# Re-ordering the split of x1, two VectorE slots and the start-up transfers in a fused attention and FFN kernel

## Chip, cores and metric

The kernel runs on one core of a Trainium2 chip. The metric is the device time of one execution in microseconds (us); the median of three executions is 2120.65 us, with a lowest of 2120.45 and a highest of 2123.52.

## The reference

The input `x` has shape (2, 4096, 512), all in float32. One attention-like layer is followed by one FFN, and each is followed by a residual sum and a layer norm.

```python
k = rope((x @ Wk.T) in 16 heads of 32);  v = (x @ Wv.T) in 16 heads of 32
W = eye(32) for each batch and head
for each chunk of 16 tokens:            # 256 chunks, one after the other
    z = kc @ W
    W = W - kc.T @ (z - vc) * 2 / (16 * 32)
out = (layernorm(z) * gamma + beta) @ Wo.T
x1  = layernorm(x + out)
h   = silu((x1 @ gate_w.T) * gate_s) * ((x1 @ up_w.T) * up_s)     # 1408 wide
y   = layernorm(x1 + (h @ down_w.T) * down_s)
```

## The kernel before

**Tiles, ticks, slots.** The 4096 positions are cut into 32 tiles of 128; a tile holds both batches (256 tokens) and 8 chunks. The program is a software pipeline with the order of every engine written out by hand. `run` calls `tick(t)` for t = -1 to 35 on each engine, and a tick has 16 slots `s`. In tick t the engines work on several tiles: keys and values of tile t (and, from slot 7 on, of tile t + 1), the scan of tile sc = t - 1, norm, output projection and x1 of tile o = t - 2, and the FFN of tiles f1 = t - 2 (slots 14 and 15) and f2 = t - 3 (slots 0 to 13). Every engine takes its instructions in program order, and semaphores tie the engines together.

**The scan.** In an even slot TensorE makes z of a chunk (`scan_z`, 32 small matmuls), VectorE subtracts v (`scan_err`, 4 instructions), in the odd slot TensorE adds to the state in PSUM (`scan_state`, 16 matmuls) and ScalarE copies the state out (`keep_state`, 4 instructions). ScalarE also saves z (`save_z`).

**The split into two parts.** A float32 operand is split into a rounded high part (ScalarE, `high_x`, `high_zn`, `high_x1`, `high_hid`) and the remainder (VectorE `low_x`, `low_zn`, `low_x1`; GpSimd `low_hid`). A projection (`project_k`, `project_v`, `project_o`, 12 matmuls of 512 columns) is high times high, high times low and low times high. The FFN weights are small integers, so the FFN takes two products, if the low halves of all its weights are zero: `weigh` reduces 12 pieces of the weights to a maximum on VectorE, GpSimd reduces over partitions in tick 2, and TensorE reads the result before it goes on at slot 14 of tick 2.

**The FFN.** Eleven steps m per tile: `gate_up` (16 matmuls of 256 columns into the bank `gu_acc`), ScalarE `gate` (silu), VectorE `scale_hid`, ScalarE `high_hid`, GpSimd `low_hid`, then `down` (4 matmuls of 512 columns). There is one bank `gu_acc`, so `gate_up` of step m waits for `scale_hid` of step m - 1. Step 0 is in slot 14 and needs both parts of x1 (`x1_lo_ready`); it is where a tile's FFN begins.

**x1.** VectorE adds the projection and x in slots 7 and 8 (`add_o`), takes statistics (`stats_of`, `moments_of`), GpSimd takes the inverse root (`inverse_root`), VectorE normalizes in slot 9 and transposes 32x32 blocks (`turn_x1`), four DMAs store them and one loads them back as `landed`. In slot 13 ScalarE runs `high_x1` twice. On VectorE slot 13 reads

```python
rotate(t + 1, 0)
scale_y(yd)        # down_acc times down_scale, waits for the last down
low_x1(o, 0)
low_x1(o, 1)
```

and slot 8 reads `add_o`, `stats_of`, `scan_err`, `moments_of`, `scale_hid`. Slot 2 reads `scan_err`, `turn_zn` twice, `scale_hid`, `rotate`. The normalized z goes the same way through DRAM as x1: `turn_zn`, `store_znT`, `load_znT` (SP), `high_zn` and `low_zn` in slot 5, `project_o` in slots 6 and 7.

**The start.** The FFN weights are first copied from the inputs to DRAM scratch (three DMAs of 2816 KB, `copy_ffn`, issued by ScalarE in tick -1) and loaded in tick 1 (`load_ffn`). All four projections of tile 0 go through the one bank `work`. SP stores and loads the transposed keys (`store_kT`, `load_kT`).

## Time and profile before

| what | value |
|---|---|
| median of 3 executions | 2120.65 us |
| the profiled execution, and its span | 2128.82 us, 2126.9 us |
| TensorE busy (matmul) | 1910.0 us, 90% |
| VectorE busy | 1358.6 us, 64% |
| ScalarE, GpSimd busy | 924.4 us, 650.7 us |
| mean granted TensorE clock | 0.953 |
| slices 2 to 4 of 40: granted clock in tenths | 6, 7, 9 |

The span goes from the first to the last instruction. A granted clock of 1.00 is TensorE's full speed (2.4 GHz) and 0.50 is its lower level (1.2 GHz). The idle time in square brackets at the end of a row is that of the engine just before the instruction, with what ended it.

### The profile page before, as it was taken

Reading aid. Unit: us, or ns where it says so; the run is one execution under the profiler, and the core shown is the slowest. Engines: PE = TensorE matmul, PEld = TensorE weight load, DVE = VectorE, ACT = ScalarE, POOL = GpSimd, SP = SyncE. Lnnn points to the kernel's source line nnn. Section 1 sums busy time; section 2 is a strip of 40 time slices with the busy share of each in tenths; the row PEclk is TensorE's granted clock in tenths of the full one; section 3 lists DMA queues with packets and bytes.
Section 4 is the critical chain, followed back from the end, with each engine's and each line's share of the span. In section 5 each row is a group of like instructions: output and inputs, shape, how many; then the busy total and the mean of one; then the engine's idle time right before and its main releaser. Section 6 shows DMA issues by size and latency. Waiting matters only on the chain.

```text
span 2126.9 us, 53841 instructions
## 1 busy us (share of the span) xinstructions
PE 1910.0 (90%) x21656; PEld 1500.9 (71%) x21656; DVE 1358.6 (64%) x2878; ACT 924.4 (43%) x2258; POOL 650.7 (31%) x778
## 2 busy tenths in 40 slices
PE   5548999999999999999999999999999999998887
PEld 3326777777777777777777777777777777777665
DVE  3465676667666666676676666667666666766542
ACT  2324444444444444444444444444444444444421
POOL 1012323333333333333323323332332333333222
PEclk9679999999999999999999999999999999999998
DMA  8843444554444445444434544443454444444320
GB/s 297 266 124 117 141 120 136 152 157 127 133 138 138 131 144 155 130 143 136 142 118 142 153 149 124 137 144 116 140 153 147 125 144 138 135 122 133 94 66 21
DMA packets 307978, 294.02 MB, mean 138 GB/s; under 512 B 42896, under 2 KB 256144, under 8 KB 307728
## 3 DMA queue, kind: packets, MB, share of 16 engines
q1 hardware_dynamic: 302768, 273.26, 42.7%
q10 hardware_dynamic: 4960, 17.30, 2.2%
q8 instruction: 173, 2.83, 0.6%
q14 instruction: 77, 0.63, 0.1%
HBM read 156.19 MB, written 142.87 MB: 141 GB/s over the span
## 4 chain that ended last, share of the span: by engine, by line
PE 61%; DVE 24%; DMA 5%; issue 5%; SPq 3%; POOL 1%; ACT 1%; DVEq 0%; POOLq 0%; ACTq 0%
PE gu_acc L704 26%; PE work L690 18%; PE down_acc L716 11%; DVE err L881 7%; DVE x_lo L917 4%; PE z_acc L663 3%; PE state_acc L678 3%; DVE hid L888 2%; DVE x_tok L898 2%; SPq L252 2%; DVE turned L821 2%; DVE x_tok L816 1%; DVE stats L802 1%; DMA landed<-zT_scr 1%; DMA zT_scr<-turned 1%
## 5 line engine op out<-in xcount | busy, mean ns | idle before, releaser
L443 POOL TENSOR_TENSOR hid_lo<-hid,hid_hi 128x256 fp32r<-128x256 f32 x352 | 269.2, 765 | 1013.1 <-ACT hid_hi L534 1013.1
L704 PE MATMUL gu_acc<-x_hi,gw 128*128 128x256 f32 x1408 | 400.1, 315 | 104.3 <-DVE x_lo L917 65.8
L881 DVE TENSOR_TENSOR err<-z_acc,v_rows 32x256 f32<-32x256 f32 x1024 | 429.3, 419 | 100.9 <-PE z_acc L663 65.2
L500 ACT ACTIVATE state<-state_acc 32x256 f32<-32x256 f32 x1028 | 383.7, 373 | 111.3 <-PE state_acc L678 91.5
L704 PEld LDWEIGHTS gu_acc<-x_hi,gw 128*128 128x128 f32 x1408 | 275.0, 195 | 170.0 <-DVE hid L888 74.3
L888 DVE SCALAR_TENSOR_TENSOR hid<-gu_acc,up_scale,hid 128x256 f32<-128x256 f32 x352 | 168.9, 480 | 314.8 <-ACT hid L524 311.0
L524 ACT ACTIVATE hid<-gu_acc,gate_scale 128x256 f32<-128x256 f32 x352 | 166.6, 473 | 456.9 <-PE gu_acc L704 454.9
L704 PE MATMUL gu_acc<-x_hi,uw 128*128 128x256 f32 x1408 | 364.4, 289 | 0.0
L704 PE MATMUL gu_acc<-x_lo,uw 128*128 128x256 f32 x1408 | 363.4, 289 | 0.0
L704 PE MATMUL gu_acc<-x_lo,gw 128*128 128x256 f32 x1408 | 362.5, 288 | 0.0
L716 PE MATMUL down_acc<-dw,hid_hi 128*128 128x512 f32 x704 | 282.3, 401 | 0.9 <-POOL hid_lo L443 0.9
L704 PEld LDWEIGHTS gu_acc<-x_hi,uw 128*128 128x128 f32 x1408 | 279.2, 198 | 0.0
L716 PE MATMUL down_acc<-dw,hid_lo 128*128 128x512 f32 x704 | 279.1, 397 | 0.0
L704 PEld LDWEIGHTS gu_acc<-x_lo,uw 128*128 128x128 f32 x1408 | 278.8, 198 | 0.0
L704 PEld LDWEIGHTS gu_acc<-x_lo,gw 128*128 128x128 f32 x1408 | 277.1, 197 | 0.1
L509 ACT ACTIVATE v_rows<-z_acc 128x256 f32<-128x256 f32 x256 | 97.6, 381 | 376.9 <-DVE err L881 376.9
L690 PE MATMUL work<-wk,fm 128*128 128x512 f32 x768 | 208.5, 423 | 17.2 <-DVE fm L912 17.0
L534 ACT ACTIVATE hid_hi<-hid 128x256 fp32r<-128x256 f32 x352 | 147.0, 418 | 173.7 <-DVE hid L888 172.7
L690 PE MATMUL work<-wv,fm 128*128 128x512 f32 x768 | 205.6, 411 | 6.5 <-DVE k_sin L870 6.5
L690 PE MATMUL work<-wo,fm 128*128 128x512 f32 x768 | 196.0, 404 | 8.5 <-DVE fm L902 5.8
L690 PEld LDWEIGHTS work<-wk,fm 128*128 128x128 f32 x768 | 148.5, 200 | 59.3 <-DVE fm L912 17.8
L690 PEld LDWEIGHTS work<-wv,fm 128*128 128x128 f32 x768 | 146.0, 197 | 41.9 <-DVE k_sin L870 8.7
(64 smaller groups left out, 2122.9 us busy)
## 6 DMA issues: line engine op xcount, KB each, us to landing
x_fm<-xT SPq DMA_DIRECT2D x64, 256.0 KB, 3.5
k_scr<-k_tok SPq DMA_DIRECT2D x32, 512.0 KB, 3.4
kT_scr<-turned SPq DMA_DIRECT2D x128, 128.0 KB, 2.9
kT<-kT_scr SPq DMA_DIRECT2D x32, 512.0 KB, 3.5
k_rows<-k_scr SPq DMA_DIRECT2D x512, 32.0 KB, 2.0
v_rows<-v_scr SPq DMA_DIRECT2D x512, 32.0 KB, 2.1
z_scr<-v_rows SPq DMA_DIRECT2D x32, 512.0 KB, 3.1
z_tok<-z_scr SPq DMA_DIRECT2D x512, 32.0 KB, 1.8
```

Source lines behind the costliest of these rows:

```text
L443: pool.tensor_tensor(hid_lo[m % RING][:], hid[m % 2][:], hid_hi[m % RING][:].bitcast(F32), ALU.subtract).then_inc(hid_lo_ready, 1)
L500: act.activation(state[q, :, e].rearrange("p (r g) e -> p r g e", r=2), state_acc[q, :, 0:P].rearrange("p r (g e) -> p r g e", e=HEAD), AC ...
L509: act.activation(v_rows[:, i].rearrange("p a (r c) -> p a r c", r=2), z_acc[:, :, 0:P].rearrange("p r (a c) -> p a r c", a=2), ACT.Copy).t ...
L524: act.activation(hid[m % 2][:], gu_acc[:, 0:TOK], ACT.Silu, scale=gate_scale[:, m:m + 1]).then_inc(silu_done, 1)
L534: act.activation(hid_hi[m % RING][:], hid[m % 2][:], ACT.Copy).then_inc(hid_hi_ready, 1)
L663: mm = pe.matmul(z_acc[j * HEAD:(j + 1) * HEAD, r, odd * 2 * HEAD:(odd + 1) * 2 * HEAD], lhsT=k_cols[k, i // 2, g, i % 2, :], rhs=state[k, ...
L690: mm = pe.matmul(work[:], lhsT=fm[p_x][:, c, b, :], rhs=w[p_w][:, c, :], start=(c == 0 and k == 0), stop=(c == NC - 1 and k == 2))
L704: mm = pe.matmul(gu_acc[:, k * TOK:(k + 1) * TOK], lhsT=w[:, c, m * P:(m + 1) * P].bitcast(dt), rhs=part[:, c].bitcast(dt), start=(c == 0 ...
L716: mm = pe.matmul(down_acc[b][:], lhsT=part[m % RING][:, b * P:(b + 1) * P].bitcast(dt), rhs=dw[:, m, :].bitcast(dt), start=(m == 0 and par ...
L881: dve.tensor_tensor(err[q, g:g + 2, :, :].rearrange("p a (r h) e -> p a r (h e)", r=2), z_acc[q, :, 0:P].rearrange("p r (a c) -> p a r c", ...
L888: dve.scalar_tensor_tensor(hid[m % 2][:], gu_acc[:, TOK:2 * TOK], up_scale[:, m:m + 1], hid[m % 2][:], ALU.mult, ALU.mult).then_inc(hid_re ...
L917: dve.tensor_tensor(token_blocks(x1_lo, b), by_token(landed, b), token_blocks(x1_hi, b).bitcast(F32), ALU.subtract).then_inc(x1_lo_ready, 1)
```

## The change

It has six parts.

1. x1: `high_x1` moves from slot 13 to slot 12 on ScalarE; on VectorE `low_x1(o, 0)` moves to slot 12 and `low_x1(o, 1)` stands behind `rotate` and ahead of `scale_y` in slot 13.
2. Slot 8 of VectorE: `scan_err` goes ahead of `stats_of`, and `moments_of` goes behind `scale_hid`. The order is then `add_o`, `scan_err`, `stats_of`, `scale_hid`, `moments_of`.
3. Slot 2 of VectorE: `turn_zn(o, 1)` goes behind `scale_hid`.
4. FFN weights: gate and up are copied in rows of a quarter of the length (1408 instead of 5632 bytes); only the gate copy is issued in tick -1, up and down follow in slot 9 of tick 0; the loads of gate and up are cut by block of 128 rows. In tick 1 the gate is loaded in slots 1 and 3, up in 9 and 11, down in 13. The pieces of `weigh` move, and the last reduction moves from slot 13 to slot 11 of tick 2.
5. Tile 0: its four projections use the banks `work`, `gu_acc`, `down_acc[0]` and `down_acc[1]` and do not wait for each other's readers. ScalarE stores and loads its transposed keys (`turn_first_k`).
6. Ticks before 3: a projection is cut into two halves in two slots.

Left out of the diff are the lines that only pass the bank on in `project`, `rotate` and `copy_v`.

```diff
-WEIGHED = {(1, 11): (0,), (1, 13): (1,), (1, 15): (2,), (2, 1): (3,), (2, 3): (4, 5), (2, 5): (6, 7), (2, 9): (8,),
-           (2, 11): (9, 10), (2, 12): (11,)}
+WEIGHED = {(1, 9): (0,), (1, 11): (1,), (1, 13): (2,), (1, 15): (3,), (2, 1): (4, 5), (2, 3): (6, 7), (2, 5): (8,),
+           (2, 9): (9, 10), (2, 10): (11,)}
+PARTS = 4
+EARLY_TICKS = 3
+HALF_UNITS = {1: (0, 2), 2: (2, NC)}
...
-        gw_scr = nc.dram_tensor("gw_scr", [DM, INTER], F32, kind="Internal").ap()
-        uw_scr = nc.dram_tensor("uw_scr", [DM, INTER], F32, kind="Internal").ap()
+        gw_scr = nc.dram_tensor("gw_scr", [PARTS, DM, INTER // PARTS], F32, kind="Internal").ap()
+        uw_scr = nc.dram_tensor("uw_scr", [PARTS, DM, INTER // PARTS], F32, kind="Internal").ap()
...
+        def k_bank(n, b):
+            return down_acc[0] if n == 0 and b == 1 else work
+
+        def v_bank(n, b):
+            return (gu_acc, down_acc[1])[b] if n == 0 else work
+
...
-                if within(t):
+                if within(t) and t >= 1:
                     store_kT(t)
...
                     load_z(sc, 0, NS // 2, 16)
+                if within(t) and t >= 1:
+                    load_kT(t)
                 if within(t):
-                    load_kT(t)
                     load_k_half0(t)
...
-                    if t == 2 and s == 13:
+                    if t == 2 and s == 11:
...
             def copy_ffn(i):
-                dst, src = ((gw_scr, gwT), (uw_scr, uwT), (dw_scr, dwT))[i]
-                act.dma_start(dst.rearrange("(c p) n -> p c n", p=P), src.rearrange("(c p) n -> p c n", p=P)
-                              ).then_inc(ffn_copied[i], 16)
-
-            def load_ffn(i):
-                dst, src = ((gw, gw_scr), (uw, uw_scr), (dw, dw_scr))[i]
+                if i < 2:
+                    act.dma_start((gw_scr, uw_scr)[i], (gwT, uwT)[i].rearrange("r (k n) -> k r n", k=PARTS)
+                                  ).then_inc(ffn_copied[i], 16)
+                else:
+                    act.dma_start(dw_scr.rearrange("(c p) n -> p c n", p=P), dwT.rearrange("(c p) n -> p c n", p=P)
+                                  ).then_inc(ffn_copied[i], 16)
+
+            def load_ffn(i, c0=0, c1=NC):
                 act.wait_ge(ffn_copied[i], 16)
-                act.dma_start(dst[:].bitcast(F32), src.rearrange("(c p) n -> p c n", p=P)).then_inc(ffn_in[i], 16)
+                if i < 2:
+                    for c in range(c0, c1):
+                        act.dma_start((gw, uw)[i][:, c, :].bitcast(F32).rearrange("p (k n) -> p k n", k=PARTS),
+                                      (gw_scr, uw_scr)[i][:, rows(c)].rearrange("k p n -> p k n")
+                                      ).then_inc(ffn_in[i], 16)
+                else:
+                    act.dma_start(dw[:].bitcast(F32), dw_scr.rearrange("(c p) n -> p c n", p=P)).then_inc(ffn_in[i], 16)
+
+            def turn_first_k():
+
+                act.wait_ge(k_turned, 2)
+                for a in range(HQ):
+                    act.dma_start(kT_scr[:, :, a].rearrange("h d g t -> d h (g t)"),
+                                  turned[a * HEAD:(a + 1) * HEAD].rearrange("d h g t -> d h (g t)")).then_inc(kT_stored, 16)
+                act.wait_ge(kT_stored, 64)
+                act.dma_start(kT[:].rearrange("p a g t -> p (a g t)"),
+                              kT_scr.rearrange("h d a g t -> (h d) (a g t)")).then_inc(kT_in, 16)
...
                         high_x(t + 1, s - 7)
-                    if within(o) and s == 13:
+                    if within(o) and s == 12:
...
-                        for i in range(3):
-                            copy_ffn(i)
+                        copy_ffn(0)
                     if t == 0 and s == 9:
...
+                        turn_first_k()
+                        copy_ffn(1)
+                        copy_ffn(2)
...
-                    if t == 1 and s in (3, 5, 9):
-                        load_ffn((3, 5, 9).index(s))
+                    if t == 1 and s in (1, 3):
+                        load_ffn(0, s - 1, s + 1)
+                    if t == 1 and s in (9, 11):
+                        load_ffn(1, s - 9, s - 7)
+                    if t == 1 and s == 13:
+                        load_ffn(2)
...
                 pe.wait_ge(wo_in, 16 * NC)
+                pe.wait_ge(k_mul, 6)
...
-            def project_k(n, b):
-                pe.wait_ge(x_low, 2 * n + b + 1)
-                if b == 1:
-                    pe.wait_ge(v_ready, 2 * n + 1)
-                elif n >= 3:
-                    pe.wait_ge(o_added, 2 * (n - 2))
-                elif n >= 1:
-                    pe.wait_ge(v_ready, 2 * n)
-                project(b, wk, k_projected, split=0 if n == 0 and b == 0 else None)
+            def project_k(n, b, c0, c1):
+                if c0 == 0:
+                    pe.wait_ge(x_low, 2 * n + b + 1)
+                    if n >= 1 and b == 1:
+                        pe.wait_ge(v_ready, 2 * n + 1)
+                    elif n >= 3:
+                        pe.wait_ge(o_added, 2 * (n - 2))
+                    elif n >= 1:
+                        pe.wait_ge(v_ready, 2 * n)
+                project(b, wk, k_projected, c0, c1, split=0 if n == 0 and b == 0 else None, acc=k_bank(n, b))
             def project_v(n, b, c0, c1):
-                if c0 == 0:
+                if c0 == 0 and n >= 1:
                     pe.wait_ge(k_mul, 6 * n + 3 * b + 3)
-                project(b, wv, v_projected, c0, c1, split=NC if n == 0 and b == 0 else None)
+                project(b, wv, v_projected, c0, c1, split=NC if n == 0 and b == 0 else None, acc=v_bank(n, b))
...
-                    if within(t) and s == 1:
-                        project_k(t, 1)
-                    if within(t) and s == 4:
+                    if within(t) and t >= EARLY_TICKS and s == 1:
+                        project_k(t, 1, 0, NC)
+                    if within(t) and t >= EARLY_TICKS and s == 4:
                         project_v(t, 1, 0, NC)
+                    if within(t) and t < EARLY_TICKS and s in (1, 2):
+                        project_k(t, 1, *HALF_UNITS[s])
+                    if within(t) and t < EARLY_TICKS and s in (4, 5):
+                        project_v(t, 1, *HALF_UNITS[s - 3])
                     if t == 0 and s == 5:
...
                         project_o(o, s - 6)
-                    if within(t + 1) and s == 12:
-                        project_k(t + 1, 0)
+                    if within(t + 1) and t >= EARLY_TICKS and s == 12:
+                        project_k(t + 1, 0, 0, NC)
+                    if within(t + 1) and t < EARLY_TICKS and s in (11, 12):
+                        project_k(t + 1, 0, *HALF_UNITS[s - 10])
                     if within(f2) and s in LATE_DOWN:
...
                     if within(t + 1) and s in (13, 14):
-                        project_v(t + 1, 0, *((0, 3), (3, NC))[s - 13])
+                        c = 3 if t >= EARLY_TICKS else 2
+                        project_v(t + 1, 0, *((0, c), (c, NC))[s - 13])
...
                 w, c0, c1 = PIECES[piece]
-                dve.wait_ge(ffn_in[piece // NC], 16)
+                dve.wait_ge(ffn_in[piece // NC], 16 * NC if piece < 2 * NC else 16)
                 dve.tensor_reduce(low_half[:, piece:piece + 1],
...
                         add_o(o, s - 7)
+                    if within(sc) and s % 2 == 0:
+                        scan_err(sc, s // 2)
+                    if within(o) and s in (7, 8):
                         dve.wait_ge(o_added, 2 * o + s - 6)
                         stats_of(1, s - 7, x_tok)
-                    if within(sc) and s % 2 == 0:
-                        scan_err(sc, s // 2)
-                    if within(o) and s == 8:
-                        moments_of(1, o)
                     if within(yn) and s == 0:
...
                         turn_zn(o, 0)
-                        turn_zn(o, 1)
                     if within(o) and s == 5:
...
                         low_x(t + 1, 1)
+                    if within(o) and s == 12:
+                        low_x1(o, 0)
                     if within(t + 1) and s == 13:
                         rotate(t + 1, 0)
+                    if within(o) and s == 13:
+                        low_x1(o, 1)
                     if within(yd) and s == 13:
                         scale_y(yd)
-                    if within(o) and s == 13:
-                        low_x1(o, 0)
-                        low_x1(o, 1)
                     if within(yd) and s == 15:
...
                         normalize(0, o, z_tok, z_tok, zn_ready)
+                    if within(o) and s == 8:
+                        moments_of(1, o)
+                    if within(o) and s == 2:
+                        turn_zn(o, 1)
                     if within(t) and s == 2:
...
                         weigh(piece)
-                    if t == 2 and s == 13:
+                    if t == 2 and s == 11:
                         dve.wait_ge(low_half_max, len(PIECES))
...
                                           ).then_inc(low_half_max, 1)
```

## Rows read from the trace of the kernel before

**Rows 1.** Who waited for whom, TensorE, whole span: us in total, times, longest.

```profile
PE gu_acc L704 <- DVE x_lo L917: 65.8, 31, 4.4
...
PE gu_acc L704 <- DVE hid L888: 36.5, 65, 2.0
```

**Rows 2.** Timeline of TensorE, the first matmuls of gate_up: start us, us, what.

```profile
237.66 0.38 PE L704 MATMUL gu_acc<-x_hi,gw 128*128 128x256 f32 x1 [1.96 <-DVE x_lo L917]
...
299.52 0.42 PE L704 MATMUL gu_acc<-x_hi,gw 128*128 128x256 f32 x1 [1.96 <-DVE x_lo L917]
...
423.17 0.39 PE L704 MATMUL gu_acc<-x_hi,gw 128*128 128x256 f32 x1 [1.96 <-DVE x_lo L917]
...
426.40 0.39 PE L704 MATMUL gu_acc<-x_hi,gw 128*128 128x256 f32 x1
...
483.57 0.39 PE L704 MATMUL gu_acc<-x_hi,gw 128*128 128x256 f32 x1 [1.96 <-DVE x_lo L917]
...
1036.74 0.39 PE L704 MATMUL gu_acc<-x_hi,gw 128*128 128x256 f32 x1 [1.96 <-DVE x_lo L917]
...
1041.44 0.39 PE L704 MATMUL gu_acc<-x_hi,gw 128*128 128x256 f32 x1
...
1901.08 0.39 PE L704 MATMUL gu_acc<-x_hi,gw 128*128 128x256 f32 x1 [1.97 <-DVE x_lo L917]
```

**Rows 3.** Stretches: us, busy PE, PEld, DVE, ACT, POOL, granted clock, DMA.

```profile
423.10:426.50 3.40, 3.33 (x36) 2.65 (x36) 2.24 (x7) 0.97 (x3) 0.00 (x0) 1.00 0.11 37
1036.80:1040.20 3.40, 3.40 (x17) 3.40 (x18) 1.49 (x4) 0.38 (x1) 0.00 (x0) 0.53 0.13 41
```

**Rows 4.** Timeline, all engines, slots 12 and 13; the first x_lo.

```profile
167.46 1.29 DVE L917 TENSOR_TENSOR x_lo<-landed,x_hi 128x512 fp32r<-128x512 f32 x2 [1.43 <-ACT x_hi L566]
...
1028.76 0.38 ACT L509 ACTIVATE v_rows<-z_acc 128x256 f32<-128x256 f32 x1 [1.73 <-DVE err L881]
...
1029.90 0.69 DVE L865 TENSOR_TENSOR k_tok<-work,rot 128x512 f32<-128x512 f32 x1 [1.18 <-PE work L690]
...
1032.14 2.26 PE L690 MATMUL work<-wv,fm 128*128 128x512 f32 x9
...
1032.96 1.15 ACT L566 ACTIVATE x_hi<-landed 128x512 fp32r<-128x512 f32 x2
...
1033.63 3.06 DVE L917 TENSOR_TENSOR x_lo<-landed,x_hi 128x512 fp32r<-128x512 f32 x2
```

**Rows 5.** Timeline, VectorE and TensorE, slots 8 to 10 of that tick.

```profile
1015.87 0.17 DVE L810 TENSOR_SCALAR var_eps<-moments 128x2 f32<-128x2 f32 x1
1016.07 0.48 DVE L888 SCALAR_TENSOR_TENSOR hid<-gu_acc,up_scale,hid 128x256 f32<-128x256 f32 x1
1016.92 1.43 DVE L816 TENSOR_SCALAR x_tok<-x_tok,moments,rstd 128x512 f32<-128x512 f32 x2 [0.37 <-POOL rstd L421]
...
1019.49 0.44 DVE L888 SCALAR_TENSOR_TENSOR hid<-gu_acc,up_scale,hid 128x256 f32<-128x256 f32 x1
...
1020.00 0.39 PE L704 MATMUL gu_acc<-x_hi,gw 128*128 128x256 f32 x1
```

**Rows 6.** Slots 2 to 6: two timeline rows, one DMA row (KB, us to landing).

```profile
1003.92 1.43 PE L690 MATMUL work<-wo,fm 128*128 128x512 f32 x5
...
1060.07 0.34 SPq L324 DMA_DIRECT2D landed<-zT_scr  x1
...
landed<-zT_scr SPq DMA_DIRECT2D x32, 512.0 KB, 3.7
```

**Rows 7.** Timeline of the first ticks, ScalarE, VectorE and TensorE.

```profile
37.42 1.15 ACT L559 ACTIVATE fm<-x_fm 128x512 fp32r<-128x512 f32 x2 [7.50 <-DMA x_fm<-xT]
...
57.07 1.31 DVE L881 TENSOR_TENSOR err<-z_acc,v_rows 32x256 f32<-32x256 f32 x3 [11.57 <-DMA v_rows<-v_scr]
...
59.60 5.15 PE L690 MATMUL work<-wk,fm 128*128 128x512 f32 x12
...
121.48 1.77 DVE L881 TENSOR_TENSOR err<-z_acc,v_rows 32x256 f32<-32x256 f32 x4
...
174.66 0.68 PE L663 MATMUL z_acc<-state,k_cols 64*32 64x64 f32 x32 [6.22 <-issue]
```

More of the change, by code:

```diff
@@ L541, in copy_v @@
                     act.wait_ge(k_ready, 2 * n + 2)
-                act.activation(v_tok[b][:], work[:], ACT.Copy).then_inc(v_ready, 1)
+                act.activation(v_tok[b][:], v_bank(n, b)[:], ACT.Copy).then_inc(v_ready, 1)
             def high_zn(n, b):
@@ L682, in scan_state, with project @@
                             mm.then_inc(state_added, 1)
-            def project(b, w, done, c0=0, c1=NC, split=None):
+            def project(b, w, done, c0=0, c1=NC, split=None, acc=work):
                 for c in range(c0, c1):
@@ L689, in project @@
                     for k, (p_x, p_w) in enumerate(((0, 0), (0, 1), (1, 0))):
-                        mm = pe.matmul(work[:], lhsT=fm[p_x][:, c, b, :], rhs=w[p_w][:, c, :],
+                        mm = pe.matmul(acc[:], lhsT=fm[p_x][:, c, b, :], rhs=w[p_w][:, c, :],
                                        start=(c == 0 and k == 0), stop=(c == NC - 1 and k == 2))
@@ L862, in rotate @@
                 heads = DM // HEAD
-                k_in = work[:].rearrange("p (h a d) -> p h a d", a=2, d=HEAD // 2)
+                acc = k_bank(n, b)
+                k_in = acc[:].rearrange("p (h a d) -> p h a d", a=2, d=HEAD // 2)
                 k_si = k_sin[:].rearrange("p (h a d) -> p h a d", a=2, d=HEAD // 2)
                 dve.tensor_tensor(k_tok[:, b, :].rearrange("p (h d) -> p h d", d=HEAD),
-                                  work[:].rearrange("p (h d) -> p h d", d=HEAD),
+                                  acc[:].rearrange("p (h d) -> p h d", d=HEAD),
                                   rot[n % 2][:, 0:1, :].to_broadcast([P, heads, HEAD]), ALU.mult).then_inc(k_mul, 1)
```

## The prediction

> **What bounds the kernel now.** I read the page first: TensorE is busy 90% of the span, the chain that ended last is 61% TensorE and 24% VectorE, and the granted clock is near full except in slices 2 to 4. So there are two places to look: what interrupts TensorE in the 28 regular tiles, and the first three ticks, where it is half idle. The waits give the first [rows 1]: 31 waits for `x_lo`, one per tile from tick 3 on, and 65 short ones for `scale_hid`. The timeline shows the first wait as a constant: 1.96 us at every regular tile [rows 2]. From 237.66 to 1901.08 there are 27 intervals, 61.61 us on average. Most are long (299.52 - 237.66 = 61.86), 8 are short (483.57 - 423.17 = 60.40). The stretches tell why [rows 3]: behind the wait the clock is 0.53 in the long tick and 1.00 in the short one. Step 0 of `gate_up` and what stands between it and step 1 take 426.40 - 423.17 = 3.23 us at full speed and 1041.44 - 1036.74 = 4.70 us at the lower level [rows 2], 1.47 us more. A long tick thus pays 1.96 + 1.47 us for a late `x_lo`.
>
> **x1 split ahead of the scaling (part 1).** `x_lo` is late because it stands behind `scale_y`, which waits for the last `down`, and then takes 3.06 us for two instructions beside GpSimd's residual sum, against 1.29 us for the first pair in the trace [rows 4]. In the new order `high_x1` follows the save of z (1028.76 + 0.38) and is half done at about 1029.8, so `low_x1(o, 0)` costs 0.65 us just ahead of `rotate`, which moves from 1029.90 to about 1030.5. Its three instructions end near 1031.8, and their reader, the next projection, starts at 1032.14 [rows 4]: cost nothing, with 0.3 us to spare. If the instruction takes 1.53 us (half of 3.06), that projection is 0.6 us late; this is the upper bound, 16 us in 27 ticks. `low_x1(o, 1)` follows, ends between 1032.5 and 1033.9, and `gate_up` may start at 1036.74 - 1.96 = 1034.78. The wait is gone, and `scale_y` and its reader on GpSimd, 0.1 to 0.9 us later, are needed only by statistics 3 us behind. What is late next: `scan_err` of slot 14 is free at 1034.8, the silu of step 0 follows it, and step 1 starts 3.23 us after step 0 as in the short tick. So step 1 moves from 1041.44 to 1038.01. Gain: 3.43 us in a long tick, 1.96 in a short one. Moved DMAs: none; SP's store of the last z comes earlier by the earlier `scan_err`.
>
> **Slot 8 (part 2).** Now `scale_hid` ends at 1016.55, TensorE has waited for it (one of the two short waits per tile [rows 1], some 0.56 us), and VectorE itself idles 0.37 us for GpSimd's inverse root before it normalizes at 1016.92 [rows 5]. From the end of `var_eps` (1016.04) to `normalize` are 0.88 us, of which `scale_hid` fills 0.48. In the new order `scale_hid` comes before `moments_of`, about 0.6 us sooner, and nothing stands in the 0.88 us. VectorE's chain from `add_o` to `scale_hid` of slot 9 has the same work and 0.48 us more idle. That next `scale_hid` ended at 1019.93, and its reader, `gate_up` in slot 10, started at 1020.00 without a wait: cover 0.07 us [rows 5]. It will start at 1020.48. TensorE wins 0.56 us at slot 9 and waits about 1.04 us at slot 10: a loss of 0.48 us per tick. The other bound is that the 0.56 us stay (gain 0.56); it would need slack in slot 9 that the rows don't have.
>
> The Trainium skill (TensorE: Matmul & The Clock Gate, section Architectural detail) says that ScalarE and VectorE are strictly first in, first out, and only TensorE's weight loads are pulled ahead. By that rule nothing of slot 9 can slip into the 0.88 us, and the sum is a loss of 0.48; if VectorE could reorder, it would be a gain of up to 0.56. The rows don't contradict it: VectorE idles 0.37 us ahead of `normalize` with other work behind.
>
> **Slot 2 (part 3).** `scale_hid` comes one transpose (0.65 us) sooner, and TensorE's 0.52 us wait goes; the second transpose ends 0.45 us later and `rotate` does not move. But the transposed z goes through DRAM: SP loads it at 1060.07, it lands 3.7 us later [rows 6] at 1063.77, and with about 1.35 us for `high_zn` and `low_zn` (half of 1.15, half of 1.29, latency) its reader can start at 1065.1. The reader started at 1003.92, in the next tick 1065.78. After the change it is ready at 1065.6 and wanted at 1065.26: 0.35 us of the 0.52 come back as a wait. I take a gain of 0.15 (bounds -0.3 and 0.52).
>
> **Regular ticks.** 60.40 - 1.96 + 0.48 - 0.15 = 58.77 us, for long and short alike. Against 61.61 that is 2.84 x 27 = 77 us; some 5 us of the 27 intervals are late DMAs, which I leave in: 72 us. Tick 3's own wait with its clock gives 3 us more. The last three tiles hold 65.8 - 28 x 1.96 = 10.9 us of the waits [rows 1], plus 3 x 1.47 of clock, less 2 x 1.15 us because `high_x1` now stands ahead of `keep_state` where TensorE has no projection to cover it: 13 us.
>
> **Start (parts 4 to 6).** The first `scan_err` is at 57.07 after 11.57 us of waiting for `v_rows`, and `high_x` of tile 1 waited 7.50 us for `x_fm` until 37.42, both behind the weight copies [rows 7]. With one copy of three ahead of them and four banks, keys and values of tile 0 are done some 4 us sooner and the transposed keys are not stored behind 5.6 MB. ScalarE, though, waits for those stores itself, and behind it stand the high parts of Wo, VectorE's `low_part` and `rotate(1, 0)`. I put the first `scan_err` near 44, a gain of 13 us (bounds 7.5, and the two waits, 19). A whole projection at the low clock is 5.15 us [rows 7] with 1.8 us of VectorE work beside it, 3.4 us bare; two halves leave 2 x 0.8. That is 1.8 us for each of eight in ticks 1 and 2; where VectorE is the bound (tick 2's second `scan_err` waits until 121.48 for statistics and a weight piece [rows 7]) it hides, so 6 us (0 to 14). The wait of 6.22 us ahead of 174.66 [rows 7] is for the reduction over all weights; two slots earlier it is done in time: 6 us (0 to 6.22). The moved pieces: one more (1.6 us) ahead of tick 2's second `scan_err`, one less later; a first piece in slot 9 of tick 1 may wait for a gate that lands only then: minus 1 (minus 6 to 0). Sum 24 us, bounds 5 and 38.
>
> On the shorter rows the Trainium skill (DMA: Bandwidth & Descriptors, section Queues, rings and completion order) says that a DMA engine takes turns between queues packet by packet. By that rule a shorter row on ScalarE's queue makes SP's transfers land sooner, by my estimate 5 us more in ticks 1 and 2. If bytes alone counted, nothing beyond the above. The 7.50 us wait fits both, so the sum leaves it out.
>
> **Sum.** 72 + 3 + 13 + 24 = 112 us. The profiled execution, 2128.82 us with a span of 2126.9, becomes 2017; the median of the runs shown stands 8.2 us below it, so 2120.65 - 112 = 2009 us. A difference of 0.2% (4 us) is about what a measurement can tell.
>
> **Rivals.**
> - A, slot 8 gains: the 0.56 us stay and no 0.48 is lost. 27 x 1.04 = 28 us, 1981 us. Against it: 0.07 us of cover. Chance 0.12.
> - B, the clock still falls: the 1.04 us wait in slot 10 and the smaller ones leave TensorE at the lower level once per tick. For it: the short ticks show that a 1.96 us wait does not decide alone. Price 19 to 27 ticks x 1.47 = 28 to 40 us, 2043 us. Chance 0.15. The Trainium skill (the same clock page, section What's actually happening) has the clock set by how busy TensorE was recently, not by one gap, which is this rival's rule.
> - C, the start gives nothing: transfers in tick 1 now meet the up and down copies, VectorE waits for weight pieces. 2033 us. Chance 0.12.
> - D, slower: `low_x1(o, 0)` waits for x1's landing and blocks `rotate` and the next projection. It landed at 1032.96 at the latest [rows 4]; then the projection starts at 1035.8 instead of 1032.14, and with the clock's 1.47 us a tick is 58.77 + 3.7 + 1.47 = 63.9 us: 27 x 2.3 = 62 us lost, less 24 + 16, about 2143 us. It decides from a landing some 1 us ahead of that bound (112 / 27 = 4.1 us per tick, 1.47 of it clock). Against it: ScalarE did not wait for a DMA there. Chance 0.03.
>
> **Chances and range.** The forecast (2009, its own range 1992 to 2026) has 0.58. From 1975 to 2047 lie all but D and tails of A and B. Faster 0.96, within 0.2% 0.01, slower 0.03.
>
> **What would show it.** No `x_lo` wait and clock 1.00 behind slot 14; intervals of 58.8 us; a wait for `scale_hid` near 1 us once per tile in slot 10, none in slots 3 and 9; some 0.35 us waits for `low_zn`; the first `scan_err` near 44 us; FFN start near 151 instead of 175 us. I am wrong if intervals are below 58 (slot 8 gained), near 60.3 (clock), or if `rotate` waits for `x_hi`.

## The result, and the profile after

The changed kernel takes 2068.96 us (median of 4 executions, 2065.99 to 2073.80) against 2121.94 us (median of 4, 2120.45 to 2123.52): a ratio of 0.9748, interval 0.9729 to 0.9767. It is 53 us faster, and the forecast was 112 us faster: the time lies above the range of 1975 to 2047. The profiled execution took 2071.61 us with a span of 2069.7, which is 57.2 us less than the profiled execution before.

First the page of the changed kernel, its slices: TensorE's busy share, the granted clock in tenths, the DMA share.

```profile
span 2069.7 us, 53846 instructions
...
PE   3235999999999999999999999999999999999887
...
PEclk8677999999999999999999999999999999999999
DMA  5574444454555444544544445445444454444320
...
```

and two lines of the page before:

```profile
PE   5548999999999999999999999999999999998887
...
DMA  8843444554444445444434544443454444444320
```

The start is thinner than before: in its first four slices TensorE is busy 3, 2, 3 and 5 tenths, where it was 5, 5, 4 and 8, and the DMA share starts at 5 and 5 tenths instead of 8 and 8. What becomes of the waits of [rows 1] stands in the view of who waited for whom (us in total, times, longest):

```profile
PE work L725 <- DVE k_sin L914: 56.9, 3, 53.9
PE state_acc L713 <- DVE err L925: 42.0, 16, 16.3
PE gu_acc L739 <- DVE hid L932: 30.9, 42, 1.4
PE work L725 <- DVE fm L946: 24.5, 25, 2.7
```

The `x_lo` wait is gone entirely. The waits for `scale_hid` fell from 65 to 42, the waits for the low part of z rose from 6 to 25 (24.5 us in all), and one wait of 53.9 us stands alone at the top. The line of the kernel before for the low part of z is

```profile
PE work L690 <- DVE fm L902: 5.8, 6, 1.8
```

To place them, the timeline of TensorE, the rows that answer to [rows 2] and [rows 6]: the FFN start of tile 1 (its first `gate_up`, in slot 14 of tick 3), then a `scale_hid` wait in slot 10 and two `low_zn` waits in slot 6, and the FFN start 27 ticks later.

```profile
264.54 0.38 PE L739 MATMUL gu_acc<-x_hi,gw 128*128 128x256 f32 x1
...
645.90 3.06 PE L725 MATMUL work<-wo,fm 128*128 128x512 f32 x12 [1.57 <-DVE fm L946]
...
662.25 0.39 PE L739 MATMUL gu_acc<-x_hi,gw 128*128 128x256 f32 x1 [0.77 <-DVE hid L932]
...
764.26 4.61 PE L725 MATMUL work<-wo,fm 128*128 128x512 f32 x12 [1.97 <-DVE fm L946]
...
1860.19 0.39 PE L739 MATMUL gu_acc<-x_hi,gw 128*128 128x256 f32 x1
```

These rows split the 57.2 us. The 27 intervals between 264.54 and 1860.19 average 59.10 us (before 61.61): 67.8 us gained. From 1860.19 to the span's end are 209.5 us (before 225.8): 16.3 gained. But tick 3's FFN starts at 264.54 instead of 237.66: **26.9 us lost** where 27 were to be gained. 67.8 + 16.3 - 26.9 = 57.2. The regular part came nearly as forecast; the start came 54 us short. (The 54 us between the medians of the changed kernel and experiment 1 are another number, which is split there.)

The timeline of the start, DMA issues of ScalarE (ACTq) and then the first `high_part` of Wo, VectorE's `low_part`, the projection behind them and the first `scan_err` (other rows of that stretch left out):

```profile
25.23 19.00 ACTq L600 DMA_DIRECT2D kT_scr<-turned  x1
44.26 1.44 ACTq L600 DMA_DIRECT2D kT_scr<-turned  x3
52.72 0.35 ACTq L603 DMA_DIRECT2D kT<-kT_scr  x1
53.12 0.64 ACTq L580 DMA_DIRECT2D uw_scr<-uwT  x1
53.79 25.66 ACTq L583 DMA_DIRECT2D dw_scr<-dwT  x1
79.49 2.19 ACT L515 ACTIVATE wo<-x_tok 128x512 fp32r<-128x512 f32 x4 [51.86 <-issue]
...
80.16 2.50 DVE L891 TENSOR_TENSOR wo<-x_tok,wo 128x512 fp32r<-128x512 f32 x4 [49.85 <-ACT wo L515]
...
84.57 5.24 PE L725 MATMUL work<-wv,fm 128*128 128x512 f32 x12 [53.85 <-DVE k_sin L914]
...
90.35 1.77 DVE L925 TENSOR_TENSOR err<-z_acc,v_rows 32x256 f32<-32x256 f32 x4 [5.83 <-PE z_acc L698]
```

Read it from below. The first `scan_err` is at 90.35 (before 57.07 [rows 7], forecast 44). The projection ahead of it waited 53.85 us for `rotate(1, 0)`, which stands on VectorE behind `low_part`, which waited 49.85 us for `high_part` of Wo, which stood behind 51.86 us without compute on ScalarE. In them one store of the transposed keys took 19.00 us to issue and one copy 25.66; from 45.70 to 52.72 ScalarE waited for the four stores to land, before it could load the keys. What held them shows in the stretches (columns as in [rows 3], the last two the DMA share and GB/s):

```profile
39.00:44.20 5.20, 0.00 (x0) 0.00 (x0) 0.00 (x0) 0.00 (x0) 0.00 (x0) 0.50 0.29 102
60.00:70.00 10.00, 0.00 (x0) 0.00 (x0) 0.00 (x0) 0.00 (x0) 0.00 (x0) 0.50 0.27 96
```

and the same view of the kernel before, while its copies ran:

```profile
20.00:30.00 10.00, 8.35 (x48) 5.74 (x47) 2.69 (x5) 1.19 (x2) 1.29 (x1) 1.00 0.98 343
```

In these stretches the old copies kept 0.98 of the 16 DMA engines busy, the new ones about a quarter (0.27), at 96 instead of 343 GB/s. The new access pattern of gate and up is (k r n) with k = 4 outermost. The Trainium skill (DMA: Bandwidth & Descriptors, section Why a DMA increments its semaphore by 16 and not by 1) says that a transfer is spread over the largest number of engines up to 16 that divides the slowest dimension of both access patterns. The trace agrees: 4 of 16 is 0.25, and the share measured is 0.27; experiment 2 shows where the 4 that the program writes does not decide.

### The profile page after: what moved, and what is told of

It reads as the page before. It is cut to its first block, busy times and chain, and to the rows that moved or that the text cites. A ratio compares the mean times of both kernels' runs of the same rounds, so it can differ in the third digit from the quotient of the medians.

```text
span 2069.7 us, 53846 instructions
## 1 busy us (share of the span) xinstructions
PE 1869.2 (90%) x21656; PEld 1460.7 (71%) x21656; DVE 1300.4 (63%) x2878; ACT 914.4 (44%) x2258; POOL 641.1 (31%) x778
## 4 chain that ended last, share of the span: by engine, by line
PE 47%; DVE 24%; DMA 11%; issue 7%; SPq 4%; ACT 3%; POOL 2%; ACTq 1%; DVEq 0%; POOLq 0%
PE work L725 18%; PE gu_acc L739 16%; DVE err L925 9%; PE down_acc L751 8%; DMA landed<-zT_scr 5%; DMA zT_scr<-turned 4%; DVE hid L932 3%; DVE turned L864 3%; PE z_acc L698 2%; DVE stats L845 2%; DVE x_tok L859 2%; PE state_acc L713 2%; POOL rstd L431 2%; SPq L307 2%; SPq L261 2%
## 5 line engine op out<-in xcount | busy, mean ns | idle before, releaser
L739 PE MATMUL gu_acc<-x_hi,gw 128*128 128x256 f32 x1408 | 386.3, 307 | 34.0 <-DVE hid L932 30.9
L739 PE MATMUL gu_acc<-x_lo,gw 128*128 128x256 f32 x1408 | 348.1, 280 | 0.0
L739 PE MATMUL gu_acc<-x_hi,uw 128*128 128x256 f32 x1408 | 347.5, 280 | 0.0
L739 PE MATMUL gu_acc<-x_lo,uw 128*128 128x256 f32 x1408 | 346.9, 279 | 0.0
L739 PEld LDWEIGHTS gu_acc<-x_hi,gw 128*128 128x128 f32 x1408 | 265.3, 188 | 98.9 <-DVE hid L932 74.9
L739 PEld LDWEIGHTS gu_acc<-x_lo,gw 128*128 128x128 f32 x1408 | 266.0, 189 | 0.1
L739 PEld LDWEIGHTS gu_acc<-x_hi,uw 128*128 128x128 f32 x1408 | 265.0, 188 | 0.0
L739 PEld LDWEIGHTS gu_acc<-x_lo,uw 128*128 128x128 f32 x1408 | 264.8, 188 | 0.0
L725 PE MATMUL work<-wv,fm 128*128 128x512 f32 x744 | 196.9, 407 | 56.9 <-DVE k_sin L914 56.9
L725 PE MATMUL work<-wo,fm 128*128 128x512 f32 x768 | 200.2, 411 | 25.9 <-DVE fm L946 24.5
L725 PEld LDWEIGHTS work<-wo,fm 128*128 128x128 f32 x768 | 144.2, 194 | 62.1 <-DVE fm L946 28.1
```

Source lines behind the costliest of these rows:

```text
L725: mm = pe.matmul(acc[:], lhsT=fm[p_x][:, c, b, :], rhs=w[p_w][:, c, :], start=(c == 0 and k == 0), stop=(c == NC - 1 and k == 2))
L739: mm = pe.matmul(gu_acc[:, k * TOK:(k + 1) * TOK], lhsT=w[:, c, m * P:(m + 1) * P].bitcast(dt), rhs=part[:, c].bitcast(dt), start=(c == 0 ...
```

## The experiments

The theory, S: the outermost 4 puts the copies on a quarter of the engines, and ScalarE, which issues behind them, hangs and keeps Wo's high parts back. The rival L: the shorter rows (1408 bytes) make the copies slow. A second rival: ScalarE hangs because of the keys' transfers that it got. Each experiment starts from the changed kernel unless it says otherwise. Times are medians, ratios are to the kernel before in the same session; starts and intervals come from the one profiled execution of each. "Interval" is the mean over the 27 ticks. Eight of the kernels (the changed one and experiments 1, 2, 3, 4, 5, 11 and 12) run the same code in these ticks, and their intervals go from 58.66 to 59.21 us, which is 15 us in all; their shortest interval is 58.01 to 58.05 in each. So a difference of some 0.5 us between two mean intervals shows nothing by itself.

**1. Rows of the same length, the other order.**

```diff
-act.dma_start((gw_scr, uw_scr)[i], (gwT, uwT)[i].rearrange("r (k n) -> k r n", k=PARTS))
+act.dma_start((gw_scr, uw_scr)[i].rearrange("k r n -> r k n"),
+              (gwT, uwT)[i].rearrange("r (k n) -> r k n", k=PARTS))
```

> Edit: the gate and up copies keep their rows of 1408 bytes and their layout, but the access pattern runs over the 512 matrix rows first and over the 4 quarters second, not over the 4 quarters first. Theory S (spread): in the trace of after the DMA engines are 0.27 to 0.29 busy while only these copies run, a quarter of 16 engines, because the outermost dimension is 4; the copies take long, and ScalarE hangs in the issue of what follows them. Then the two long issues (19.0 and 25.7 us) go, the copies run at about 0.99 DMA share as before, the first scan_err is near 44 us instead of 90.35, the first gate_up near 151 us instead of 205, and the time is about 2069 - 54 = 2015 us. Theory Q (queue order): the transposed keys on ScalarE's queue stand behind the gate copy whatever its spread; then the first gate_up stays above 185 us and the time above 2045. Theory L (row length): rows of 1408 bytes give four times the descriptors and these fill the queue; no change, 2069 us.

2014.99 us, ratio 0.9516 (0.9483 to 0.9548): 54 us less than the changed kernel, with the same bytes and rows. Timeline of ScalarE and VectorE in this kernel:

```profile
31.66 5.14 ACTq L583 DMA_DIRECT2D dw_scr<-dwT  x1
36.84 2.19 ACT L515 ACTIVATE wo<-x_tok 128x512 fp32r<-128x512 f32 x4 [9.17 <-issue]
...
47.16 1.77 DVE L925 TENSOR_TENSOR err<-z_acc,v_rows 32x256 f32<-32x256 f32 x4 [5.30 <-PE z_acc L698]
```

and its stretches:

```profile
39.00:44.20 5.20, 2.28 (x5) 1.82 (x6) 2.87 (x6) 0.03 (x1) 1.96 (x3) 0.50 1.07 374
```

The issues are short, the engines full at 374 GB/s, the first `scan_err` is at 47.16, tick 3's FFN starts at 219.50 (gain 18.2 where 27 was forecast), the interval is 58.67. Between the two profiled executions lie 60.0 us: 45.0 of them are in the start, 11.5 in the regular ticks, which the edit doesn't touch, and 3.5 behind them. So what the order of the dimensions is shown to cost is the 45 us of the start. The forecast had the first `scan_err` at 44 and tick 2's FFN start at 151; they are at 47.16 and 159.41. L falls: rows of 1408 bytes copy at full rate.

**2. Long rows, outermost 4, in one contiguous block.** The scratch is [DM, INTER] again and the loads read whole rows, the pattern names 4 blocks of 128 rows:

```diff
+act.dma_start((gw_scr, uw_scr)[i].rearrange("(k r) n -> k r n", k=PARTS),
+              (gwT, uwT)[i].rearrange("(k r) n -> k r n", k=PARTS))
```

> Edit: gate and up are copied in whole rows of 5632 bytes, a quarter as many pieces, but with an outermost dimension of 4 (4 blocks of 128 rows). Theory S: the copies still run on a quarter of the DMA engines, DMA share near 0.27 while they run alone, and the start stays late: first gate_up within 10 us of 205, 2060 to 2075 us. Whether ScalarE still hangs in the issue shows whether the number of pieces fills the queue; the copies' own duration stays. Theory L: a quarter of the pieces frees the queue, both long issues go and the first gate_up is near 151 us, 2015 us.

2021.37 us, ratio 0.9525 (0.9506 to 0.9545). S as I had put it fails here: the pattern says 4, and tick 2's FFN starts at 162.80, as if the copies ran on all engines, which this stretch shows:

```profile
39.00:44.20 5.20, 4.24 (x43) 2.94 (x41) 0.00 (x0) 0.60 (x1) 0.77 (x3) 0.69 0.89 276
```

The four blocks touch each other, so that the pattern can be written as fewer, longer dimensions. With the 4 of the program the rule cited above would give a quarter here too; it fits this run only if the dimensions are joined before it is applied. I narrowed S: the outermost 4 counts only where the dimensions cannot be joined. Experiment 3 tests that.

**3. Long rows, outermost 4, not joinable.** From experiment 2:

```diff
-(gw_scr, uw_scr)[i].rearrange("(k r) n -> k r n", k=PARTS)
+(gw_scr, uw_scr)[i].rearrange("(r k) n -> k r n", k=PARTS)     # the same for the source
```

> Edit: as e2_long_rows_4 (whole rows of 5632 bytes, outermost dimension 4), but the four groups are rows 0, 4, 8, ... and 1, 5, 9, ..., so the pattern is not one contiguous block. e2 ran its copies at a DMA share of 0.8 to 1.2, all engines, though its outermost dimension was 4 as written; its whole pattern was contiguous. Theory S, narrowed: an outermost dimension of 4 that can't be merged into a contiguous block keeps a copy on a quarter of the engines, whatever the row length: DMA share near 0.27, first gate_up back at 190 to 205 us, 2055 to 2070 us. Theory L (rows of 1408 bytes were the trouble): rows are long here, DMA share near 1, first gate_up near 160 us, 2015 to 2022 us.

2047.51 us, ratio 0.9642 (0.9617 to 0.9666). Its stretch with the copies alone, and ScalarE's timeline:

```profile
44.00:52.00 8.00, 0.00 (x0) 0.00 (x0) 0.00 (x0) 0.00 (x0) 0.00 (x0) 0.50 0.27 96
```

```profile
51.11 13.23 ACTq L583 DMA_DIRECT2D dw_scr<-dwT  x1
64.39 2.19 ACT L515 ACTIVATE wo<-x_tok 128x512 fp32r<-128x512 f32 x4 [36.90 <-issue]
```

Rows of 5632 bytes run at the same 0.27 and 96 GB/s as rows of 1408, and tick 2's FFN starts at 196.01. The narrowed S holds in the share and the start; the total is 8 us below its range of 2055 to 2070. With a quarter as many rows (512 instead of 2048 in a copy, each four times as long) the issue behind it is held 13.23 us instead of 25.66, and ScalarE's whole idle time is 36.90 instead of 51.86: the copies' speed is the same, the time that ScalarE hangs is not.

**4. Eight parts.** `PARTS = 8`, rows of 704 bytes, the (k r n) order kept.

> Edit: the change with 8 parts instead of 4 (rows of 704 bytes, twice as many pieces, outermost dimension 8). Theory S: the copies spread over half of the DMA engines, DMA share near 0.5 to 0.6 while they run alone against 0.27 with 4 parts, about half as long; the first gate_up between 170 and 185 us instead of 205, about 2035 us. Theory L (the number or the shortness of the pieces does it): twice the pieces are worse, first gate_up above 215 us, above 2080 us.

2042.81 us, ratio 0.9625 (0.9607 to 0.9642): the shortest rows of all, and faster than four parts. Stretches and ScalarE's timeline:

```profile
44.00:52.00 8.00, 0.00 (x0) 0.00 (x0) 0.00 (x0) 0.00 (x0) 0.07 (x1) 0.50 0.59 160
```

```profile
41.03 16.34 ACTq L583 DMA_DIRECT2D dw_scr<-dwT  x1
57.41 2.19 ACT L515 ACTIVATE wo<-x_tok 128x512 fp32r<-128x512 f32 x4 [29.55 <-issue]
```

The share is 0.59, near 8 of 16, Wo's high parts come 22 us sooner and tick 2's FFN starts at 181.29. Outermost 4, outermost 8 and experiment 1's order give 96, 160 and 374 GB/s in these stretches.

**5. The keys on SP, as before.** `turn_first_k` is not called, `store_kT` and `load_kT` run on SP for tile 0 too.

> Edit: the change as it is, but SP stores and loads tile 0's transposed keys again, as before the change; ScalarE's copies are untouched. Theory S: the up and down copies, issued at about 28 us behind the gate copy, block ScalarE in the issue, and the high parts of Wo, and so rotate(1, 0) and the first scan_err, wait for that: a first scan_err at 60 to 85 us, 2045 to 2065 us. Theory Q: the whole loss came from the keys on ScalarE's queue: the first scan_err near 45 us, first gate_up near 151 us, 2015 us.

2059.16 us, ratio 0.9695 (0.9668 to 0.9723). ScalarE's timeline:

```profile
25.55 20.82 ACTq L580 DMA_DIRECT2D uw_scr<-uwT  x1
46.41 29.87 ACTq L583 DMA_DIRECT2D dw_scr<-dwT  x1
76.33 2.19 ACT L515 ACTIVATE wo<-x_tok 128x512 fp32r<-128x512 f32 x4 [48.05 <-issue]
```

Without the keys' transfers ScalarE hangs for 50.7 us, in the issue of the copies. The second rival falls: the keys' transfers were held like whatever stood next. The first `scan_err` is at 87.61, 2.7 us sooner and just behind the 60 to 85 of theory S. FFN start in tick 2 is at 203.26 instead of 205.01, so that where they stand moved the start by 1.8 us. The profiled executions are 8.1 us apart; the rest is in the regular ticks (5.1 us, interval 58.91 against 59.10) and behind them, which this edit doesn't touch.

**6. Part 1 alone.** The kernel before, with `high_x1` in slot 12, `low_x1(o, 0)` in slot 12 and `low_x1(o, 1)` ahead of `scale_y`, and nothing else.

> Edit: the kernel before with part 1 alone (high_x1 in slot 12, low_x1 split over slots 12 and 13, ahead of scale_y). By the prediction's steps: no x_lo wait, clock 1.00 behind slot 14, every interval 60.40 - 1.96 = 58.44 us plus late DMAs; start unchanged but for 3 us. 27 x (61.61 - 58.6) + 3 + 13 = 97 us faster, about 2025 us. Rival (the wait moves): rotate waits for x_hi or the clock still falls, intervals of 60 us or more, 2060 us or more.

2028.82 us, ratio 0.9569 (0.9552 to 0.9586): 94 us less than the kernel before, from moving four instructions on two engines. The median interval is 58.43 us (forecast 60.40 - 1.96 = 58.44), the mean 58.74.

**7. Slot 8 in the old order**, and **8. slot 2 in the old order**, each on top of experiment 1:

```diff
 # 7, VectorE slot 8: add_o, stats_of, scan_err, moments_of, scale_hid
 # 8, VectorE slot 2: scan_err, turn_zn(o, 0), turn_zn(o, 1), scale_hid, rotate
```

> Edit: the kernel with the re-ordered copies (e1) with VectorE's slot 8 as before the change (add_o, stats_of, scan_err, moments_of, scale_hid). In e1 the first gate_up waits 0.70 us once per tile (slot 10) and no longer in slot 9; the shortest interval is 58.04 us and the mean of 27 is 58.67. Prediction's step (the new order costs 0.48 us per tick): intervals 0.48 shorter, shortest 57.56, 13 us faster than e1. As the waits of after show it (0.56 won, 0.70 lost): 0.14 shorter, shortest 57.90, 4 us faster. Rival A (the new order gains): intervals 0.5 us longer, 14 us slower than e1.

> Edit: the kernel with the re-ordered copies (e1) with VectorE's slot 2 as before the change (both turn_zn ahead of scale_hid). Prediction's step: a 0.52 us wait for scale_hid comes back in slot 3, and the waits of the output projection for low_zn (15 us in 16 waits in e1's regular tiles) mostly go: shortest interval 58.56, mean 0.15 longer than e1's 58.67, 4 us slower than e1. Rival (slot 2 gains its full 0.52): mean 0.5 longer, 14 us slower. Rival (slot 2 loses, the late z costs more than 0.52): faster than e1.

Experiment 7: 2007.45 us, ratio 0.9466 (0.9446 to 0.9485); 8: 2017.75 us, 0.9515 (0.9494 to 0.9536); experiment 1 had 0.9516 (0.9483 to 0.9548). Who waited for whom, TensorE, in 7:

```profile
PE gu_acc L739 <- DVE hid L932: 22.8, 38, 1.4
PE work L725 <- DVE fm L946: 21.1, 23, 2.7
```

and in 8:

```profile
PE gu_acc L739 <- DVE hid L932: 44.6, 69, 2.0
...
PE work L725 <- DVE fm L946: 3.9, 5, 1.3
```

In experiment 1 the two lines had 28.7 and 17.5 us. The old slot 2 has 16 us more of `scale_hid` waits and 14 us less of `low_zn` waits: the 0.52 us that the change wins in slot 2 it gives back in slot 6, for z must still go through DRAM. Interval 58.72 against 58.67: nothing that can be told from zero, though the shortest interval is 0.5 us longer (58.51 against 58.04). The old slot 8 shortens the shortest interval from 58.04 to 57.82 us, but the mean is 58.70 against 58.67, as the tick then runs into `low_zn` again. The ratios say 0.5% (11 us) for the old order, the medians 8 us, the profiled executions nothing (2012.74 against 2011.63); the intervals of the two ratios touch. In the traces the new order trades a wait of 0.56 us in slot 9 in each tick for one of 0.73 in slot 10. What slot 8 is worth in the total stays open between 0 and some 11 us, on the side of a loss.

**9. The second `turn_x1` behind `scale_hid`**, on top of experiment 1. `scale_hid` of slot 9 is the late one in slot 10, and it stands behind both `turn_x1`:

```diff
-                        turn_x1(o, 1)
...
+                    if within(o) and s == 9:      # behind scale_hid
+                        turn_x1(o, 1)
```

> Edit: e1, and the second turn_x1 goes behind scale_hid of slot 9 (0.65 us of transpose out of the way of the gate_up that waits 0.70 us in slot 10). Theory: the wait is VectorE's order alone; it shrinks to 0.05, the shortest interval to 57.4, 18 us faster than e1. Price: x1 is stored 0.45 us later, relative to TensorE 1.1 us; if it then lands too late for high_x1 in slot 12, low_x1 and rotate wait, the projection behind rotate waits for k_sin, and part of it is given back.

1997.09 us (1996.22 to 2001.66), ratio 0.9419 (0.9400 to 0.9438), the fastest kernel of the study. Who waited for whom in it:

```profile
PE gu_acc L739 <- DVE hid L932: 9.0, 20, 1.4
```

The wait for `scale_hid` falls from 28.7 to 9.0 us, the interval from 58.67 to 58.03 and the shortest one from 58.04 to 57.44, below that of every kernel before it. So slot 10's wait was really set by the order in slot 9, and there it could be removed.

**10. Wo's high parts ahead of two copies.** From experiment 9, `copy_ffn(1)` and `copy_ffn(2)` are issued behind Wo's `high_part`.

> Edit: e9 (re-ordered copies, second turn_x1 behind scale_hid), and ScalarE issues the up and down copies behind the high parts of Wo instead of ahead of them. In e1 the issue of the down copy held ScalarE for 5.14 us and Wo's high parts started at 36.84, so that rotate(1, 0) waited. Theory: the first scan_err comes 4 to 6 us sooner than e1's 47.16, and the rest of the start follows, 4 us faster than e9's 1997. Rival: the later copies push the weight loads into tick 2's z transfers, where VectorE already waits 10.24 us for z_tok, and nothing is left or it is slower.

2005.59 us, ratio 0.9451 (0.9437 to 0.9464) against 0.9419 (0.9400 to 0.9438) in 9: no gain, and probably a loss, as the two intervals hardly meet. The first `scan_err` comes sooner, timeline of VectorE and then of ScalarE's loads of the gate:

```profile
43.02 1.77 DVE L925 TENSOR_TENSOR err<-z_acc,v_rows 32x256 f32<-32x256 f32 x4 [6.28 <-PE z_acc L698]
```

```profile
46.00 3.69 ACTq L590 DMA_DIRECT2D gw<-gw_scr  x1
51.01 2.41 ACTq L590 DMA_DIRECT2D gw<-gw_scr  x1
53.45 2.65 ACTq L590 DMA_DIRECT2D gw<-gw_scr  x1
```

but FFN start in tick 2 is at 161.43, against 162.60 in 9: of 5.5 us at the first `scan_err` (48.48 in 9) 1.2 arrive. The issues of the gate's loads now take longer: three of the four took 2.41 to 3.69 us, in 9 all took 0.37 to 0.53. The profiled execution took 1995.11 us, the other five 2004 to 2010; no trace shows those, so why they are slower stays open.

**11. Whole projections in ticks 0 to 2** (`EARLY_TICKS = -1`) and **12. the last reduction in slot 13**, each on top of experiment 1.

> Edit: e1 without the halves: every projection of the first ticks whole again, in the slots of the kernel before. Prediction's step: the halves are worth 6 us (0 to 14): first gate_up at 165 instead of 159.4, about 2021 us. Rival: they are worth nothing, since VectorE is the bound in ticks 1 and 2: 159 to 161, 2015 us.

> Edit: e1 with the last reduction over the weights in slot 13 of tick 2 again, as before the change (VectorE's and GpSimd's part). Prediction's step: TensorE waits some 6 us for it ahead of slot 14; first gate_up at 165 us instead of 159.4, 2021 us. Rival: GpSimd's start of that instruction (4 to 5 us in the kernel before) is hidden, wait under 2 us.

Experiment 11: 2021.72 us (2014.05 to 2032.56), ratio 0.9535 (0.9500 to 0.9571). FFN start in tick 2 is at 159.51 with whole projections and 159.41 with halves: the halves win nothing there, as the rival said. The median alone would have fitted the forecast's 2021, but the two ratios overlap: two of the four executions took 2014 and 2015, near experiment 1's 2014.99, and two 2029 and 2033, of which there is no trace. Experiment 12: 2032.36 us, ratio 0.9557 (0.9537 to 0.9577). TensorE's timeline has the old wait again, the one that answers to the last row of [rows 7]:

```profile
165.41 0.68 PE L698 MATMUL z_acc<-state,k_cols 64*32 64x64 f32 x32 [6.73 <-issue]
```

FFN start is at 166.02, 6.6 us later, as forecast. The medians are 17 us apart, the profiled executions 22.5, and 14.4 of these are in the regular ticks, which the edit doesn't touch: the interval is 59.21 instead of 58.67, with four intervals above 61 us, and the waits for `low_zn` are 25.7 instead of 17.5 us. The changed kernel too has 24.5 us of them and 59.10. From one start to another the same code thus runs its regular ticks up to 0.5 us apart. What sets whether z comes in time I didn't find.

## Why the prediction was wrong

- **Part 1, right.** Forecast: the 1.96 us wait and the clock's 1.47 us gone, interval 58.44. Measured alone: 58.43, and no `x_lo` wait. The clock: over the 27 ticks the mean granted clock is 1.00 where it was 0.98, and the stretch behind the FFN start in the changed kernel is at full speed, which answers to both rows of [rows 3]:

```profile
1860.20:1863.60 3.40, 3.35 (x45) 2.67 (x37) 2.35 (x6) 0.90 (x3) 1.30 (x2) 1.00 0.12 37
```

- **Slot 8, right in place, too large in size.** The wait for `scale_hid` moved to slot 10 and is 0.69 to 0.92 us once per tick, 0.75 in the mean (forecast 1.04); the one of slot 9 is gone. Net loss by the shortest intervals 0.22 us, not 0.48.
- **Slot 2, right in place, too small in size.** "0.35 us of the 0.52 come back": about all came back. The changed kernel has waits for `low_zn` of 0.2 to 2.4 us in 23 of the 27 ticks, 20.8 us or 0.77 per tick; in experiments 1 and 8 it was 14 us back for 16 won. With both slots the median interval is 58.72 us in the changed kernel (forecast 58.77). The mean of 59.10 comes from five intervals of 60.05 to 61.71 us, each with a `low_zn` wait in it; I had allowed 5 us for late DMAs over all ticks. Rival B lives only there: behind three of these waits (1.97 us at 764.26, 1.69 at 1119.92, 2.04 at 1415.74) the clock fell to the lower level for a while and the 12 matmuls took 4.61, 4.61 and 4.31 us instead of 3.06.
- **Start, the step that failed.** "I put the first `scan_err` near 44, a gain of 13 us": it was at 90.35, a loss of 33. Its premise, "keys and values of tile 0 are done some 4 us sooner", held: the last store of the values is issued at 25.17 instead of 29.94. What failed comes behind it. The keys were to be nearly free of the copies ("the transposed keys are not stored behind 5.6 MB"), but their load is issued at 52.72 (before 47.70, experiment 1 30.63), and Wo's high parts start at 79.49 (before 40.05, experiment 1 36.84). I priced the copies by their bytes and their number ahead of the stores, taking for granted that each copy would still run on all 16 engines, and asked of the shorter rows only how they share a queue. The new order of the dimensions was not priced at all. I had written that "behind it stand the high parts of Wo, VectorE's `low_part` and `rotate(1, 0)`", and that was the path that the loss took. With the order of dimensions put right (experiment 1) the total is 2014.99 us against the 2009 forecast. That it comes so near is partly luck: between the profiled executions the start gains 18.2 us (forecast 27), the regular ticks 79.2 (72) and the last tiles 19.8 (13), misses of opposite sign. And the bounds of the start's sum, by its own terms, are 1.5 and 39, not 5 and 38; neither pair reaches a loss.
- **Start, the other terms**, by experiment 1: the first `scan_err` 9.9 us sooner (forecast 13), the earlier reduction 6.6 (6), the halves 0 (6); tick 2's FFN start 15.9 us sooner (24). The halves hide: with them TensorE's wait for tick 2's second `scan_err` ends at 112.55, with whole projections at 114.54, and by the next output projection (127.11 and 126.80) nothing is left of the 2 us, below. The forecast had named VectorE as the cover there and counted 6 us all the same. Whether shorter rows let SP's transfers land sooner, the 5 us that it left out of its sum, stays open: experiments 1 and 2 have short and long rows with all engines at work and FFN starts of 159.41 and 162.80, but their loads and issues differ too. Timeline of TensorE, experiment 1:

```profile
112.55 0.68 PE L713 MATMUL state_acc<-err,k_rows 64*32 64x128 f32 x16 [13.43 <-DVE err L925]
...
127.11 4.59 PE L725 MATMUL work<-wo,fm 128*128 128x512 f32 x12 [0.97 <-issue]
```

and experiment 11:

```profile
114.54 0.68 PE L713 MATMUL state_acc<-err,k_rows 64*32 64x128 f32 x16 [11.10 <-DVE err L925]
...
126.80 4.51 PE L725 MATMUL work<-wo,fm 128*128 128x512 f32 x12 [0.97 <-issue]
```
- **The last tiles** gained 16.3 us (forecast 13).
- **Rivals.** C (the start gives nothing, 2033 us) had the right place with a bound far too mild: it let the start give 0, not -27. B's 2043 us lies nearer to the measured time, but its cause is not what made the time. A and D are out: no interval is below 58.03, and `rotate` waits for nothing. `low_x1(o, 0)` ahead of it does wait for `high_x1`, up to 1.0 us in each tick, and the next projection covers it.

## What to carry to other kernels

When a DMA's access pattern changes, look at its outermost dimension that cannot be joined with the next, not only at bytes and row length: 4 there meant a quarter of the DMA engines, and swapping two dimensions gave back 45 us at the start. The slow transfers cost here through the engine that issued the next one: look at what compute stands behind that issue in program order. When two kernels with the same loop differ by 0.5 us per iteration, compare the shortest iterations too, before you credit the edit. And a wait found once per tile with the clock's fall behind it (1.96 + 1.47 us) was worth 94 us alone, of the 108 that all parts give in experiment 1; the short waits moved around the tick until the order was right in the one slot that set them (experiment 9).

## What the runs showed of the hardware that was not expected

- Blocks that touch are spread over all engines even where the program writes an outermost 4 (share 0.89 at 276 GB/s in experiment 2), blocks that don't are not (0.27 at 96 GB/s in experiment 3). Who joins the dimensions, the compiler or the chip, no run here tells.
- The issue of a DMA can hold ScalarE for up to 29.87 us when copies on few engines are under way. At the same transfer rate it took 25.66 us with copies of 2048 short rows and 13.23 with 512 long ones. With all engines at work the same issue took 5.14 us with 2048 rows (experiment 1) and 0.62 with 512 (experiment 2). So both count, the engines and the number or length of the rows; no run parts the last two.
- In the changed kernel the granted clock fell behind waits of 1.69, 1.97 and 2.04 us ahead of slot 6 (mean 0.64 to 0.67 over the next 12 matmuls, 4.31 to 4.61 us), and not behind waits of 1.95 us (1654.04) and 2.38 us (1060.12), where they took 3.06 and 3.07 us. As with the short and long ticks of [rows 3], the wait's length alone doesn't decide.
